# A macaron block with two expert layers: turns moved beside small sums, down products ahead of q, k, v, and half of the second experts' w2 in two parts

## The reference

```python
x = L0_attn_q_x                                              # (8, 512, 256)
x = x + 0.5 * _L0_ffn_ref(_layernorm(x), w_switch, b_switch, w1, b1, w2, b2)
x = x + _L0_attn_ref(_layernorm(x), ln1_w, ln1_b, wq, bq, ..., proj_w, proj_b)
x = x + 0.5 * _L0_ffn_ref(_layernorm(x), w_switch, b_switch, w1, b1, w2, b2)

# experts: 8 of them, 256 places each; a token goes to its best expert while there is place
logits = x @ w_switch + b_switch;  probs = softmax(logits)
slot = where(pos < capacity, routes * capacity + pos, E * capacity)
h = relu(einsum('ecd,edh->ech', buf_e, w1) + b1[:, None, :])     # hidden size 1024
y = einsum('ech,ehd->ecd', h, w2) + b2[:, None, :]
out = where(keep, y_flat[slot], x) * (pmax / pmax)

# attention: 16 heads of 16 numbers; the sums run over the heads of one token
xn = _ln(x, ln1_w, ln1_b);  q, k, v = xn @ wq + bq, xn @ wk + bk, xn @ wv + bv
fq, fk = elu(q) + 1, elu(k) + 1
kv = einsum('bhnd,bhne->bnde', fk, v);  qkv = einsum('bhnd,bnde->bhne', fq, kv)
attn = qkv / (einsum('bhnd,bnd->bhn', fq, fk.sum(axis=1)) + 1e-6)
x = x + attn @ wo + bo
return x + gelu(_ln(x, ln2_w, ln2_b) @ fc_w + fc_b) @ proj_w + proj_b   # hidden size 1024
```

## Time and profile before

| what | value |
|---|---|
| time, median of 3 (lowest to highest) | 749.41 us (749.32 to 749.81) |
| the profiled execution, its span | 749.47 us, 747.7 us |
| mean granted clock of TensorE | 0.969 |
| busy: PE, PEld | 688.8 us (92%), 582.3 us (78%) |
| busy: DVE, ACT, POOL | 450.3 us (60%), 401.3 us (54%), 315.8 us (42%) |
| down products of the middle, 768 matmuls | 107.9 us |
| up products of the middle, 384 matmuls | 104.5 us |
| plain down products of the experts, 256 records each | 60.1 us and 60.1 us |

### The profile page before, as it was taken

One profiled execution on the slowest core, in us unless ns is written; L12 is line 12 of the kernel. 1 busy time (PEld: TensorE's weight loads), 2 busy tenths in 40 slices (PEclk: granted clock), 3 DMA queues, 4 the chain that ended last, 5 costly groups with the idle time before them and its releaser, 6 DMA issues.

```text
span 747.7 us, 17265 instructions
## 1 busy us (share of the span) xinstructions
PE 688.8 (92%) x6254; PEld 582.3 (78%) x6254; DVE 450.3 (60%) x1243; ACT 401.3 (54%) x809; POOL 315.8 (42%) x462
## 2 busy tenths in 40 slices
PE   7689999997787999999999999999999867999994
PEld 5457999984566788888888888888888754999993
DVE  7863746414576666767777868677666465444430
ACT  5763555512234667676766666767654543444430
POOL 5240574222222353444563745645538454234311
PEclk9779999999999999999999999999999987999997
DMA  8486677304666444544555455444434233566610
GB/s 268 145 267 207 209 261 243 127 29 104 103 105 100 86 67 87 93 84 68 110 75 114 81 97 108 84 89 83 85 68 141 99 101 99 169 194 195 212 57 28
DMA packets 283745, 92.43 MB, mean 124 GB/s; under 512 B 213677, under 2 KB 281380, under 8 KB 283662
## 3 DMA queue, kind: packets, MB, share of 16 engines
q1 hardware_dynamic: 267310, 82.26, 45.1%
q0 software_dynamic: 3840, 8.32, 3.5%
q10 hardware_dynamic: 12512, 0.76, 1.0%
HBM read 61.95 MB, written 29.40 MB: 122 GB/s over the span
## 4 chain that ended last, share of the span: by engine, by line
PE 58%; issue 4%; DVE 4%; ACT 3%; POOL 2%; DMA 2%; SPq 2%; ACTq 2%; POOLq 0%; DVEq 0%
PE bank L1638 52%; PE bank L1650 5%; ACTq L354 2%; SPq L348 1%; DMA qkv_rows<-feats 1%; POOL hids L742 1%; ACT hids L967 1%; POOL table L626 1%; ACT feats L937 0%; ACT ots L990 0%; DMA keys<-qkv_rows 0%; DMA mid_rows<-xa_fin,xa_slot 0%; DMA x<-mid_rows 0%; ACT kvt_ L954 0%; DVE rb_stat L1050 0%
## 5 line engine op out<-in xcount | busy, mean ns | idle before, releaser
L1638 PE MATMUL bank<-down_w,hids 128*128 128x256 f32 x768 | 107.9, 285 | 1.3 <-POOL hids L742 1.3
L742 POOL TENSOR_TENSOR hids<-hid,hids 128x512 fp32r<-128x512 f32 x64 | 83.1, 1298 | 54.8 <-ACT hids L967 54.6
L1638 PE MATMUL bank<-hnts,up_w 128*128 128x512 f32 x384 | 104.5, 407 | 0.0
L1638 PEld LDWEIGHTS bank<-down_w,hids 128*128 128x128 f32 x768 | 97.4, 188 | 4.9 <-POOL hids L742 2.9
L1638 PE MATMUL bank<-qkv_w,xnts 128*128 128x256 f32 (+1 forms) x384 | 76.8, 347 | 3.8 <-DVE xnts L1501 2.9
L1638 PEld LDWEIGHTS bank<-hnts,up_w 128*128 128x128 f32 x384 | 67.6, 189 | 11.5
L1638 PEld LDWEIGHTS bank<-qkv_w,xnts 128*128 128x128 f32 x384 | 61.0, 190 | 15.8 <-DVE xnts L1501 5.1
L964 ACT ACTIVATE hid<-bank,cols 128x512 f32<-128x512 f32 x64 | 44.0, 687 | 47.5 <-PE bank L1638 47.2
L733 POOL TENSOR_SCALAR sth<-sth 128x1 f32<-128x1 f32 x32 | 7.2, 225 | 132.6 <-DVE sth L1513 132.6
L1638 PE MATMUL bank<-a_w,xa_h 128*128 128x256 f32 x256 | 60.1, 379 | 0.0
L1638 PE MATMUL bank<-b_w,xb_h 128*128 128x256 f32 x256 | 60.1, 379 | 0.0
(11 more groups left out here) (275 smaller groups left out, 1470.2 us busy)
## 6 DMA issues: line engine op xcount, KB each, us to landing
qkv_rows<-feats SPq DMA_DIRECT2D x32, 384.0 KB, 3.3
a_raw<-in_L_ffn_w_dram SPq DMA_DIRECT2D x32, 256.0 KB
a_w<-in_L_ffn_w_dram SPq DMA_DIRECT2D x32, 256.0 KB
b_raw<-in_L_ffn_w_dram SPq DMA_DIRECT2D x32, 256.0 KB
b_w<-in_L_ffn_w_dram SPq DMA_DIRECT2D x32, 256.0 KB
mid_rows<-x_all SPq DMA_DIRECT2D x8, 512.0 KB
x<-mid_rows SPq DMA_DIRECT2D x32, 128.0 KB, 2.5
values<-qkv_rows SPq DMA_DIRECT2D x32, 128.0 KB
```

The source lines that it names most:

```text
L742: pool.tensor_tensor(hids[1][u % 3][:], hid[u % 2][:], f32(hids[0][u % 3][:]), ALU.subtract).then_inc(s_hidl, 1)
L1638: return pe.matmul(dst, left, right, start=start, stop=stop, skip_group_check=True)
```

## The change

1. **Middle, order of TensorE alone.** In a step the even up product comes before zn's turn, which so stands beside the sums of k and v. The odd down products come before q, k, v. The odd up product comes before hn's turn, which so stands beside the sums with the queries.
2. **Last expert's outputs by halves**, in both layers. The second output tile has a bank of its own (bank 5). The last two pairs are done together, all of the first tile and then all of the second, each with its own count, and `finish` waits for each alone. TensorE's idle products before the middle wait for the last outputs, as they write bank 5.
3. **Second experts: half of w2 in two parts** (`SPLIT` = 2). For pairs 0 and 1, ScalarE casts w2's pair (`w2p`) and the hidden rows (`hs`), VectorE subtracts the low parts (`low_weights`, `low_hidden`), and `down` uses `product`. SP's load of w2 waits for the cast of the pair before. The counts of `high1`, `low1` and `relu` include the new operations (`parts_made`, `relus_made`).
4. Rows are gathered four experts ahead, not three, and four semaphores for loaded pieces become two.

```diff
@@ experts, sizes and counts
+            split = SPLIT if second else 0
+            w2p = [tiles(stack, f"{name}_w2p{b}", 2, [P, 2 * SPLIT, D], F32R) for b in range(2)] if second else None
+            hs = [tiles(stack, f"{n}_hs{b}", SPLIT, [P, 2, CAP], F32R) for b in range(2)] if second else None
-                rows=tiles(stack, f"{n}_rows", 3, [P, ST, D]),
+                rows=tiles(stack, f"{n}_rows", ROWS_AHEAD, [P, ST, D]),
+        def parts_made(x, c, second):
+            return x * PAIRS + max(x - E, 0) * SPLIT + c + (min(c, SPLIT) if x >= E else 0) + 1 + second
+        def relus_made(u, whole):
+            x, j = divmod(u, PAIRS)
+            split = max(x - E, 0) * SPLIT + (min(j + whole, SPLIT) if x >= E else 0)
+            return 2 * (u + 1) + split
+        def out_bank(x, s, ex):
+            if x == ex.end - 1 and s == 1:
+                return bank[5][:, 0:D]
+            return bank[2 + x % 2][:, s * D:(s + 1) * D]
@@ SP, load_weights
+                if x > ex.first and c < ex.split:
+                    sp.wait_ge(ex.sem.high1, parts_made(x - 1, c, True))
@@ GpSimd, run_experts
-                load_rows(ex.first + 2, ex)
+                for x in range(ex.first + 2, ex.first + ROWS_AHEAD):
+                    load_rows(x, ex)
@@ ScalarE, high_weights and relus
+                if c < ex.split:
+                    act.wait_ge(ex.sem.got2[c], 16 * (x + 1))
+                    if x >= ex.first + 2:
+                        act.wait_ge(ex.sem.down, (x - 2) * PAIRS + c + 1)
+                    act.copy(ex.w2p[0][x % 2][:, 2 * c:2 * c + 2], ex.w2s[x % 2][:, 2 * c:2 * c + 2]).then_inc(ex.sem.high1, 1)
+                if j < ex.split:
+                    act.wait_ge(ex.sem.relu, relus_made(u, False))
+                    act.copy(ex.buf.hs[0][j][:], ex.buf.h[u % 4][:]).then_inc(ex.sem.relu, 1)
@@ VectorE
+                if c < ex.split:
+                    pair = slice(2 * c, 2 * c + 2)
+                    dve.wait_ge(ex.sem.high1, parts_made(x, c, True))
+                    dve.tensor_tensor(ex.w2p[1][x % 2][:, pair], ex.w2s[x % 2][:, pair], f32(ex.w2p[0][x % 2][:, pair]),
+                                      ALU.subtract).then_inc(ex.sem.low1, 1)
+            def low_hidden(u, ex):
+                j = u % PAIRS
+                dve.wait_ge(ex.sem.relu, relus_made(u, True))
+                dve.tensor_tensor(ex.buf.hs[1][j][:], ex.buf.h[u % 4][:], f32(ex.buf.hs[0][j][:]),
+                                  ALU.subtract).then_inc(ex.sem.hlow, 1)
@@ VectorE, finish
+                    if x == ex.end - 1:
+                        dve.wait_ge(ex.sem.down, (x + 1) * PAIRS - 1 + s)
@@ VectorE, run_experts
+                    if u > ex.first * PAIRS and (u - 1) // PAIRS < ex.end and (u - 1) % PAIRS < ex.split:
+                        low_hidden(u - 1, ex)
@@ TensorE, down
+                if j < ex.split:
+                    pe.wait_ge(ex.sem.low1, parts_made(x, j, True))
+                    pe.wait_ge(ex.sem.hlow, (x - ex.first) * ex.split + j + 1)
+                        if j < ex.split:
+                            last = product(out, (ex.buf.hs[0][j][:, i, rows], ex.buf.hs[1][j][:, i, rows]),
+                                           (ex.w2p[0][x % 2][:, m], ex.w2p[1][x % 2][:, m]), False, m == KE - 1)
+            def down_last(x, ex):
+                pairs = (PAIRS - 2, PAIRS - 1)
+                for s in range(ST):
+                    for m in range(2 * pairs[0], KE):
+                        last = mm(out_bank(x, s, ex), ex.buf.h[(x * PAIRS + m // 2) % 4][:, m % 2, s * P:(s + 1) * P],
+                                  ex.w2s[x % 2][:, m], stop=m == KE - 1)
+                    last.then_inc(ex.sem.down, 1)
@@ TensorE, middle
+            pe.wait_ge(xa.sem.fin, E * ST)
             idle_products(8)
+                if 0 <= g_up < NG:
+                    up_mid(g_up, 2 * j_up)
                 n = at(s, 2)
...
                     turn_free = (s_xnl, n + 1)
-                if 0 <= g_up < NG:
-                    up_mid(g_up, 2 * j_up)
...
+                if 0 <= g_down < NG:
+                    down_mid(g_down, 2 * j_down + 1)
                 if at(s, 2) is not None and s != 4:
                     qkv(s - 2, v_free)
                     v_free = (s_val, s - 1)
-                if 0 <= g_down < NG:
-                    down_mid(g_down, 2 * j_down + 1)
...
+                if 0 <= g_up < NG:
+                    up_mid(g_up, 2 * j_up + 1)
                 n = at(s, 6)
...
                     turn_free = (s_hnl, n + 1)
-                if 0 <= g_up < NG:
-                    up_mid(g_up, 2 * j_up + 1)
```

83 lines of the change are left out of this document (49 added, 34 removed).

## The result

The kernel after takes 769.91 us (median of 4 runs, 768.11 to 772.9), the kernel before 749.61 on the same chip (749.32 to 752.84, 4 runs): ratio 1.0265, 95% interval 1.0221 to 1.0308. Forecast were 767 us and a range of 752 to 773. The profiled execution took 772.9 us with a span of 771.2, 3.0 above its median; the mean granted clock is 0.963 where it was 0.969.

A forecast was written before the change was run, and what follows sets the result against it. TensorE was taken to set the pace of attention steps and second experts, output sends the experts' ends. 22.1+0.5-3.3+0.7+0.5-2.6 = +17.9 on the profiled 749.47 us gave 767 us, range 752 to 773.

The forecast's parts named there:

- T+13.4: Middle: the full attention step, counted from the start T of its even up product, takes 13.4 us where it was 12.07.
- wait one: Middle: TensorE idles before the attention output's bias product until ScalarE has copied v, about 0.75 us a step.
- wait two: Middle: the even up product waits for ScalarE's cast, table load and gelus after hn's turn, about 0.55 us a step.
- The average: Middle: 24 steps of 13.5 us on average against 12.58, +22.1 us, bounds +17 to +26.
- (a): Rival, middle: one wait instead of two, as two in one step can share slack; 750 to 755 us, taken 752; 8%.
- (b): Rival, middle: gelu table load runs before hn's cast and leaves the path, joined turns spare 0.2 a step; 740 us; 10%.
- (c): Rival: the clock falls in TensorE's waits, 15 us at 1.2 GHz cost 7.5; 775 us; 7%.
- (d): Rival, second experts: VectorE or ScalarE late at each expert, the gain lost; 771 us; 5%.
- The estimate near 800: Middle: the skill's drain of about 1.38 us at each table switch would make the gelus' wait 1.4 longer, sum 33 higher.
- that for the ups: Second experts: ups fall from 1.60 to 1.45 us where both neighbours changed, half of that where one did.
- +0.7 for the start: Second experts' start: added ScalarE casts and VectorE subtractions delay the first down products, +0.7 us (0 to +2).
- Ends: Both experts' ends: the last send begins 1.28 us after its own product, -1.28 each, -2.6 us together (-1 to -3).

## Why the prediction was right, point by point

**The step.** T+13.4 for the full step was forecast, T+13.45 measured; by pieces: q, k, v at T+4.53 (4.46), bias at T+7.69 (7.65), hn's turn at T+10.03 (10.0), next up 3.42 later (3.42). The two waits by distance are 1.06-0.35 = 0.71 before the bias product (0.75) and 2.10-1.54 = 0.56 before the up (0.55). The idle notes say 0.46 and 0.40, less than the 0.5 to 0.8 that I had named as a sign for the first: they count from the modelled end of the record before, which overlaps with what could follow. Nor does the note for v stand in all steps, as I had said, but in 19 of the 23. ScalarE had 0.40 us to spare ahead of q and k, forecast 0.5. By undoing, wait one is worth 0.53 and zn's part 0.19, together 0.72, and wait two 0.71: the up behind an idle also takes 1.50 to the next turn where it takes 1.41 without, 0.09 that no term had.

**The average.** Forecast 13.5, measured 13.56 (311.8/23). The steps with turned rows, logits and counts kept to 13.4 to 13.9.

**What failed: step 10 and the way there.** I took all 24 steps alike. Step 10 took 3.0 more. This is the step of the prediction that was wrong in kind. In it the gelus come for the first time, with a table load, and there are no odd down products yet. The kernel after, then the version with the old middle:

```profile
249.57 0.58 PE L1693 MATMUL bank<-bias_rows,ones_two 128*128 128x256 f32 x1 [1.80 <-ACT feats L981]
249.94 1.48 PE L1693 MATMUL bank<-o_w,ots 128*128 128x256 f32 x6
251.22 2.31 PE L1693 MATMUL bank<-hnts,up_w 128*128 128x512 f32 x6
```
```profile
243.85 0.39 PE L1693 MATMUL bank<-bias_rows,ones_two 128*128 128x256 f32 x1 [1.09 <-ACT feats L981]
```

The wait for the copy of v is 1.80, not 1.09, and one of 0.76 for the output's low part stands ahead of it: ScalarE's load and gelus begin after zn's cast, so that here its own row of work is the bound, which for the full steps I had excluded with a margin of 0.5 us. With the clock undisturbed, as in the run with the down products moved back, step 10 takes 14.36, 1.6 more than 12.75. The other 1.4 is the clock: 0.57 from 249 to 253 us, where before has 1.00, the output products stretched from 0.71 to 1.28 us. Of the fourteen profiled executions six have zn's turn behind the up and q and k first, and in all six TensorE idles 2.6 us in step 10; in five of them the clock fell in this step, and in the sixth (the down products moved back) it didn't. It didn't either in the two with v first, which idle some 1.4 us, nor in the six with the old order. Why five and not six, nothing here shows.

The way to step 10 was 2.1 longer than in the kernel before. Between 180 and 240 us the twelve profiled executions with q and k first have none, one or two low stretches of the clock, and the way from the first zn turn to step 10 goes by their number, not by the order: 69.3 and 69.6 us with none, 69.8 to 70.7 with one, 71.6 to 72.7 with two. The kernel before had one (69.8), the kernel after two (71.95). So the +2.1 is no effect of the change that these runs show; it is part of why the profiled execution is above its median.

**Rivals.** (a) falls: the waits add. (b) was right as mechanism, since the table load is what matters, but the order doesn't give it; where I gave it, steps fell by 0.68. Its remark that the answer of q, k, v would then be hidden too was wrong: with hn's turn back, or the load early, the wait for v stayed. Its 740 needed also that joined turns save 0.2, and they save nothing. (c), the clock: it did fall, but not in the waits of the plain steps, whose stretches stay at full clock. The Trainium skill (TensorE: Matmul & The Clock Gate, A second HAM failure mode) warns of repeated short idles; the 19 waits for v and the 18 for the gelus in the steps after step 10 brought no fall here (granted clock 1.00 from 255 to 571 us). In step 10, with 2.6 us of idle between its pieces, the clock fell in five of six executions. (d) didn't come in the kernel after, and came in full with three buffers of rows.

**Table loads.** The gelu starts 0.02 us behind the load's end (267.62+1.28 to 268.92): no drain in the kernel after either. The estimate near 800 by the Trainium skill (ScalarE: Activation LUTs, What ACT_TABLE_LOAD costs) falls.

**Second experts.** -0.41 an expert forecast, -0.56 measured (13.23 to 12.67). The term for down products was right (1.54 to 1.43); that for the ups was too small, because I took the effect of the neighbours as half from each side. A group with parts ahead of it gets all of it: two groups by 0.18, which makes -0.11-0.10-0.36 = -0.57. In this place a larger gain than forecast (-4.5 for eight experts, forecast -3.3) and a low clock at the start (+1.5, below) nearly cancel, so that -4.1 against -3.9 is partly luck. +0.7 for the start was right where it can be seen: in the version with the old middle the first down in parts stands 1.10 behind its bias, before 0.32:

```profile
632.76 0.48 PE L1693 MATMUL bank<-bias_rows,ones_two 128*128 128x256 f32 x2
633.86 1.67 PE L1693 MATMUL bank<-b_w2p,xb_hs 128*128 128x256 f32 x12 [0.62 <-DVE xb_hs L1267]
```

In the kernel after it doesn't show, as the first 36 products ran partly at 1.2 GHz (0.51 from 659.0 to 662.5) and took 5.88 us, before 4.35: +1.5 in its place. Such a stretch stands there in five of the fourteen profiled executions, once with the old order, so it isn't the new order's doing alone. The w2 casts in the last middle steps and the steps without q, k, v were forecast as +1.0, and are +0.5.

**Ends.** The last send comes 1.28 after its output row, as forecast, in the kernel after too:

```profile
761.43 0.48 DVE L1307 SCALAR_TENSOR_TENSOR xb_fin<-bank,xb_scale,xb_rows 128x256 f32<-128x256 f32 x1 [1.24 <-PE bank L1693]
```
```profile
762.71 0.97 POOL L691 DMA_INDIRECT out_dram<-xb_fin,xb_slot  x1 [0.76 <-DVE xb_fin L1307]
```

At the first experts' end only 0.6 of 1.3 came in the profiled execution. I had said that it costs nothing that the idle products now wait for the outputs, as TensorE next waits for zn. Here nothing was left to cover them: the idle products ran at half clock until about 171 us, and the first zn turn followed them at once, where before TensorE had waited 2.21 us for zn. With the old order of the middle the whole 1.4 came, and TensorE waited 2.52.

So the mechanism and its price held in the steps of the middle, and step 10 was missed. In the profiled execution the sum is short by 23.5-17.9 = 5.6 us: 2.1 for step 10, 2.1 for the stretches of low clock ahead of it, 1.5 for the average step, 0.7 at the first experts' end, less 0.8 elsewhere. Against the median it is short by 2.9, and there too errors of opposite sign help: by undoing, the middle's order costs 25.2 to 27.5 us (forecast 22.6), and the rest brings 5.9 to 7.2 (forecast 4.7).

## What to carry to other kernels

Before changing the order on the busiest engine, count for each neighbour engine the answer time from its trigger to its reply, and what the busy engine has in that time; a group of products moved from inside that time to outside brings a wait of its length less the slack that was there, in each step (here 1.54 us moved, about 0.7 to spare, 0.71 waited). When an answer contains a table load, move the load ahead of its trigger by a tiny activation before moving anything else. Buffers that cost nothing may be what pays for another part of a change, and an edit that cures plain steps has to be read in the special ones too: with both waits out, most of what was left of the loss stood in the one step in which the up products begin.

## What the runs showed of the hardware that was not expected

- A group of twelve products in parts takes 1.42 us behind its own kind, also where a plain group follows, and 1.60 behind plain fp32 products.
- The same program had no stretch of some 3.5 us at 1.2 GHz in its early middle in one execution and two in another, on another chip (69.6 and 71.8 us for the same work); over twelve executions of versions with q and k first this part took 69.3 to 72.7 us, by the number of such stretches.
- In step 10, 2.6 us of idle were followed by a clock of 1.2 GHz in five of the six executions that have such an idle; why not in the sixth stays open.
- An up group behind an idle of 0.4 us takes 0.09 us longer to the next start (270.24 to 271.74, against 278.02 to 279.43 without the idle).
- A transpose beside small sums costs what it costs beside large products (2.90 and 2.92 us for the same four pieces).
